# Attention heads and key-value products of a small vision tower in 32-column array tiles, one for each pair of heads

## The reference, cut to what matters

```python
# local branch: a band of 12 tokens around each token
qk = einsum('bhsd,bhswd->bhsw', fmap(q), fmap(k_windowed))
out_local = einsum('bhsw,bhswd->bhsd', qk, v_windowed) / clip(qk.sum(-1), 1e-6)
# strided branch: every third token (the global branch: all tokens, read through 12 anchor queries)
kv = einsum('bhsd,bhse->bhde', k_s, v_s)
out_stride = einsum('bhsd,bhde->bhse', fmap(q), kv) / norm
# out = wl * out_local + ws * out_stride + wg * out_global, then a linear layer
```

## Time and profile before

| | us |
|---|---|
| median of 3 runs | 257.41 (256.68 to 260.4) |
| the profiled execution | 256.9 |
| span of its trace | 255.1 |
| attention steps 4 to 8 in the trace (66.44 to 134.97) | 68.5 |
| step 9 (134.97 to 144.10) | 9.1 |

### The profile page before, as it was taken

One profiled execution on the slowest core, in us unless ns is written; L12 is line 12 of the kernel. 1 busy time (PEld: TensorE's weight loads), 2 busy tenths in 40 slices (PEclk: granted clock), 3 DMA queues, 4 the chain that ended last, 5 costly groups with the idle time before them and its releaser, 6 DMA issues.

```text
span 255.1 us, 4433 instructions
## 1 busy us (share of the span) xinstructions
PE 219.5 (86%) x1340; PEld 189.2 (74%) x1340; DVE 141.2 (55%) x422; ACT 110.8 (43%) x252; POOL 74.7 (29%) x109
## 2 busy tenths in 40 slices
PE   7397797995999999999999773599999999999940
PEld 6286496663887967878879561489999999999930
DVE  5345248696567858657456459765776433424200
ACT  2334366864143443735326595245433424334210
POOL 4003350372004060413322363002332423324240
PEclk9659599996799999999795555579999999999996
DMA  7999999999500000000100596532342342431313
GB/s 131 188 234 159 262 291 270 265 215 255 195 10 0 0 4 1 0 3 0 31 4 26 172 318 163 134 95 49 52 59 39 57 54 37 67 44 18 31 15 89
DMA packets 26259, 25.73 MB, mean 101 GB/s; under 512 B 4971, under 2 KB 23262, under 8 KB 26222
## 3 DMA queue, kind: packets, MB, share of 16 engines
q1 hardware_dynamic: 22333, 22.17, 35.6%
q0 software_dynamic: 3568, 2.64, 8.2%
q10 hardware_dynamic: 336, 0.66, 1.5%
HBM read 16.57 MB, written 7.77 MB: 95 GB/s over the span
## 4 chain that ended last, share of the span: by engine, by line
PE 73%; DVE 8%; DMA 7%; ACT 4%; issue 3%; SPq 2%; POOL 1%; DVEq 0%; ACTq 0%; POOLq 0%
PE ps L973 12%; PE ps L950 12%; PE ps L708 7%; PE ps L712 6%; PE ps L798 5%; PE ps L580 4%; PE ps L784 4%; PE ps L962 4%; PE ps L677 4%; DMA ximg<-in_x 3%; PE ps L691 2%; PE ps L681 2%; DMA sent<-row,index 1%; PE ps L572 1%; DMA sums<-ys,xs 1%
## 5 line engine op out<-in xcount | busy, mean ns | idle before, releaser
L1640 POOL DMA_INDIRECT sums<-ys,xs x17 | 26.3, 1546 | 66.6 <-ACT ys L1537 57.1
L973 PE MATMUL ps<-w2s,hidT 128*128 x204 | 36.1, 327 | 1.1 <-DVE hidT L1341 0.8
L973 PEld LDWEIGHTS ps<-w2s,hidT 128*128 128x128 f32 x204 | 33.0, 189 | 2.1 <-issue 1.6
L950 PE MATMUL ps<-w1hi,xhi 128*128 x68 | 25.3, 372 | 1.0 <-ACT xend L1530 0.7
L1537 ACT ACTIVATE ys<-ps,xs 128x192 f32<-128x192 f32 x17 | 7.2, 421 | 39.9 <-PE ps L973 37.6
L1320 DVE TENSOR_TENSOR xlo<-ps,xhi 128x128 fp32r<-128x128 f32 x17 | 5.0, 292 | 28.2 <-ACT xend L1530 28.2
L1627 POOL COPY vexp<-vtok 114x32 f32<-114x32 f32 (+1 forms) x36 | 8.0, 222 | 42.6 <-PE ps L712 40.6
L1419 ACT ACTIVATE qlb<-ps,cst 96x228 f32<-96x228 f32 (+1 forms) x36 | 12.1, 426 | 16.8 <-PE ps L746 16.8
L1147 DVE TENSOR_TENSOR kvb<-ps,cst 96x288 f32<-96x288 f32 (+1 forms) x24 | 10.0, 418 | 16.1 <-PE ps L784 16.1
L708 PE MATMUL ps<-at,vexp 114*96 114x114 f32 (+1 forms) x144 | 18.7, 286 | 0.0
L784 PE MATMUL ps<-vm,ktok 114*96 114x288 f32 (+1 forms) x48 | 15.6, 406 | 2.7 <-DVE kvb L1147 2.7
(11 more groups left out here) (192 smaller groups left out, 473.1 us busy)
## 6 DMA issues: line engine op xcount, KB each, us to landing
w2s<-in_L_ffn_W SPq DMA_DIRECT2D x8, 576.0 KB
sent<-blank SPq DMA_DIRECT2D x1, 3977.0 KB, 32.5
w1s<-in_L_ffn_W SPq DMA_DIRECT2D x4, 768.0 KB, 16.6
xs<-sent SPq DMA_DIRECT2D x17, 96.0 KB, 2.0
w1s<-in_L_ffn_W SPq DMA_DIRECT2D x4, 384.0 KB, 18.1
w1hi<-w1hi SPq DMA_DIRECT2D x8, 192.0 KB
ximg<-in_x SPq DMA_DIRECT2D x12, 96.0 KB, 7.9
w1s<-in_L_ffn_b SPq DMA_DIRECT2D x1, 792.0 KB
```

The costliest lines, as they stand in the source:

```text
L950: last = pe.matmul(ps[2 + c][:, 0:PASS], xx, of_expert(ww, expert), start=(n == 0), stop=(n == len(products) - 1))
L973: last = pe.matmul(ps[6 + j % 2][:, 0:D], hidT[:, k, :], of_expert(w2s[:, :, k, :], expert), start=(k == 0), stop=(k == FCH - 1))
L1640: po.indirect_dma_start(sums, bass.IndirectOffsetOnAxis(ap=xs[:, j % NS, D + TAIL + 1:].bitcast(U32), axis=0), ys[:, j % 2, :], None, comp ...
```

## The change

The heads are taken in pairs: 32 channels, `PAIRS = 3` in each half of 96.

- `keys_values(g, i)`: for a half, three products instead of two. Product `r` loads the 32 key columns of pair `r`, streams the masked values of the same pair for both branches and three images (2 x 3 x 32 = 192 columns) and writes rows 32r to 32r+31 of `ps[5]`. It is issued at parts 0 and 2 of a step and no longer at parts 1 and 3. For the last group it streams 192 columns as well, where it was 96.
- `own_blocks(g, i)`: three VectorE instructions of 32 rows for a half, where there were two of 96 rows. The blocks of `kvb` outside the pairs are set to zero once, by a new GpSimd memset (`gp_blocks_zero`).
- `outputs(g, i)`: `vexp` is 32 columns wide. Six products as before, but each loads 32 columns and writes the 32 rows of its pair; the three first heads of the pairs are issued first, then the three second heads, which are summed on them. The products with `kvb` that follow stay as they are, 96 columns in the full tile.
- GpSimd fills `vexp` in two copies of 96 values instead of six of 32, and clears 768 values in place of 2304.

`scores` and the linear outputs are as they were.

```diff
+TW = 2 * HD
+PAIRS = HALF // TW
...
-        vm = sb("vm", [GTOK, 2, 2, 2 * PER, HALF])
+        vm = sb("vm", [GTOK, 2, 2, PAIRS, 2 * PER, TW])
...
-        vexp = sb("vexp", [GTOK, 2, HEADS, HALF])
+        vexp = sb("vexp", [GTOK, 2, HEADS, TW])
...
-                for hh in range(HH):
-                    pe.matmul(o, vexp[0:n, g % 2, i * HH + hh, :], at[0:n, g % 2, i * HH + hh, 0:w],
-                              start=(hh == 0), stop=False, skip_group_check=True)
+                for a in range(2):
+                    for r in range(PAIRS):
+                        hh = i * HH + 2 * r + a
+                        pe.matmul(ps[7][TW * r:TW * (r + 1), i * GTOK:i * GTOK + w], vexp[0:n, g % 2, hh, :],
+                                  at[0:n, g % 2, hh, 0:w], start=(a == 0), stop=False, skip_group_check=True)
...
-            def keys_values(g, m):
-
-                t0, n, imgs = group(g)
-                i, kind = m // 2, m % 2
+            def keys_values(g, i):
+
+                n = group(g)[1]
                 pe.wait_ge(gp_masked_values, 2 * g + i + 1)
-                if 4 * g + m >= 1:
-                    pe.wait_ge(dv_keys_values, 4 * g + m)
-                pe.matmul(ps[5][0:HALF, 0:imgs * HALF], ktok[0:n, g % KS, i * HALF:(i + 1) * HALF],
-                          vm[0:n, g % 2, i, kind * PER:kind * PER + imgs, :],
-                          start=True, stop=True).then_inc(pe_keys_values, 1)
+                if 2 * g + i >= 1:
+                    pe.wait_ge(dv_keys_values, 2 * g + i)
+                for r in range(PAIRS):
+                    c = i * HALF + r * TW
+                    last = pe.matmul(ps[5][TW * r:TW * (r + 1), 0:2 * PER * TW], ktok[0:n, g % KS, c:c + TW],
+                                     vm[0:n, g % 2, i, r].rearrange("p k c -> p (k c)"), start=True, stop=True)
+                last.then_inc(pe_keys_values, 1)
...
-                        keys_values(t - 3, m)
+                        if m % 2 == 0:
+                            keys_values(t - 3, m // 2)
                         scores(t - 3, m)
...
-                ve.tensor_tensor(kvb[:, g % 2, i, kind * PER:kind * PER + imgs, :],
-                                 ps[5][0:HALF, 0:imgs * HALF].rearrange("p (b c) -> p b c", c=HALF),
-                                 blk.unsqueeze(1).broadcast_to([HALF, imgs, HALF]), ALU.mult).then_inc(dv_keys_values, 1)
+                for r in range(PAIRS):
+                    c = slice(TW * r, TW * (r + 1))
+                    last = ve.tensor_tensor(
+                        kvb[c, g % 2, i, :, c].rearrange("p (k b) c -> p k b c", b=PER)[:, :, 0:imgs],
+                        ps[5][c, 0:2 * PER * TW].rearrange("p (k b c) -> p k b c", b=PER, c=TW)[:, :, 0:imgs],
+                        blk[c, c].unsqueeze(1).unsqueeze(1).broadcast_to([TW, 2, imgs, TW]), ALU.mult)
+                last.then_inc(dv_keys_values, 1)
...
+                    link(po.memset(kvb[:], 0.0), gp_blocks_zero)
                     link(po.memset(vexp[:], 0.0), gp_vexp_zero)
```

More of the change, by code:

```diff
@@ L406, in build @@
         gp_vexp_zero = sem("gp_vexp_zero")
+        gp_blocks_zero = sem("gp_blocks_zero")
         gp_masked_values = sem("gp_masked_values")
@@ L697, in outputs @@
                 w = max(n, HALF)
[L698 removed]
+                pe.wait_ge(dv_keys_values, 2 * g + 2)
                 pe.wait_ge(dv_windows, 4 * g + 4)
[L700 removed]
+                pe.wait_ge(gp_head_values, 2 * (g + 1))
                 pe.wait_ge(ac_from_anchors, g + 1)
@@ L1138, in over_anchors, with own_blocks @@
                                      r[:, i, :].unsqueeze(2).broadcast_to([HA, imgs, SEQ]), ALU.mult).then_inc(dv_anchored, 1)
-            def own_blocks(g, m):
-                t0, n, imgs = group(g)
+            def own_blocks(g, i):
+                imgs = group(g)[2]
                 if g >= 2:
                     ve.wait_ge(pe_heads, g - 1)
-                ve.wait_ge(pe_keys_values, 4 * g + m + 1)
-                i, kind = m // 2, m % 2
-                ve.tensor_tensor(kvb[:, g % 2, i, kind * PER:kind * PER + imgs, :],
-                                 ps[5][0:HALF, 0:imgs * HALF].rearrange("p (b c) -> p b c", c=HALF),
-                                 blk.unsqueeze(1).broadcast_to([HALF, imgs, HALF]), ALU.mult).then_inc(dv_keys_values, 1)
+                else:
+                    ve.wait_ge(gp_blocks_zero, 1)
+                ve.wait_ge(pe_keys_values, 2 * g + i + 1)
+                for r in range(PAIRS):
[5 more added lines that the diff above has]
+                last.then_inc(dv_keys_values, 1)
             def windows(g, m):
@@ L1227, in _ @@
                     if 0 <= t - 3 < GROUPS:
-                        own_blocks(t - 3, m)
+                        if m % 2 == 0:
+                            own_blocks(t - 3, m // 2)
                         windows(t - 3, m)
@@ L1625, in _ @@
                     po.wait_ge(pe_heads, g - 1)
-                for hh in range(HH):
+                for a in range(2):
                     link(po.tensor_copy(
-                        vexp[0:n, g % 2].rearrange("p (i a) c -> p i a c", i=2)[:, :, hh, hh * HD:(hh + 1) * HD],
-                        vtok[0:n, g % 3].rearrange("p (i c) -> p i c", i=2)[:, :, hh * HD:(hh + 1) * HD]), gp_head_values)
+                        vexp[0:n, g % 2].rearrange("p (r a) c -> p r a c", a=2)[:, :, a, a * HD:(a + 1) * HD],
+                        vtok[0:n, g % 3].rearrange("p (r c) -> p r c", c=TW)[:, :, a * HD:(a + 1) * HD]), gp_head_values)
             po.wait_ge(sent_blank, 16)
```

17 lines of the change are left out of this document (8 added, 9 removed).

## The result

The changed kernel takes 268.02 us, the median of four runs (266.03 to 273.94), beside 258.9 (256.68 to 263.39) for the kernel before; the ratio is 1.0388, 95% interval 1.0336 to 1.044. That is slower, and outside the range I gave. Now and then an execution comes out some per cent longer than the others of its kernel, and the ratios in this document leave such executions out, so a ratio is not always the quotient of the two medians. The profiled execution is the longest of the four, 273.94 us, with the granted clock (PEclk on the page, in tenths of full speed) at 0.50 in the first part of step 4 too; a second one (`after_again`, 265.45 us, span 263.6) stands closer to the other three, and I read the steps from it.

What follows compares the result with a forecast made beforehand. TensorE's stream was taken to bound steps 4 to 8. Terms -0.3 + 0 + 0.1 - 1.1 = -1.3 us on 256.9 gave 255.6, 256.1 as median, forecast 256; 8-in-10 range 249.5 to 266.5.

Steps and rivals of the forecast that it cites:

- The bound: Steps 4 to 8: bound by order and length of TensorE's stream, VectorE some 4 us a step behind.
- What one pass costs: Heads and key-value products: partly overlapping tiles save 0.49 us a heads block, 0.33 a key-value half, 1.64 a step.
- full overlap: Rival: second passes of heads and key-values also run side by side, 6.9 us less than forecast, 249 us; chance 0.20.
- What the tile changes cost: TensorE entering and leaving 32-column tiles: 0.29 us a visit, four visits, 1.16 us a step.
- VectorE and the new wait: Fourth `scores` waits for `windows` behind three `own_blocks`: 0.3 to 0.5 us, 0.4 taken, a step.
- Steps 4 to 7: Saving, tile changes and new wait together: -0.1 us a step, -0.3 in four.
- Step 3: TensorE's wait moves to the fourth `scores`, idle nearly 4 us in place of 2.65; nothing gained or lost.
- Steps 8 and 9: Last attention steps: +0.1 us in the first, -1.1 us in the second, which runs at half clock.
- The clock: Rival: more low-clock stretches at 3.1 us each, two giving 262.3 us, a third 265; chance 0.10.

Runs made afterwards that it cites:

- heads_only: Kernel before with only the heads in 32-column tiles (new `vexp`, copies and `outputs`), key-value products as they were: 251.0 us, ratio 0.9749.
- heads_by_pair: Kernel before with only the heads in 32-column tiles, loops exchanged so both products of one tile follow each other: 255.64 us in one run.
- keys_only: Changed kernel with `vexp`, its copies and the heads' loop as before, so only key-values are in 32-column tiles: 262.64 us, ratio 1.0163.
- after_fill6: Changed kernel with three dense products that nobody reads at the end of step 6, nothing else: 262.97 us, ratio 1.0218.
- whole_filled: Changed kernel with second half's `own_blocks` behind fourth `windows`, plus unread products: four in step 3, two ending step 6, one ending steps 7 and 8: 246.86 us.
- after_filled: Changed kernel plus unread dense products, four in step 3, one ending each of steps 6, 7, 8: 251.04, 251.69, 251.77, 267.34, 267.42 us.
- after_relit: Changed kernel with six dense products that nobody reads in step 7, behind `outputs` of the first half, no other filling: 268.96 us, ratio 1.0308.
- blocks_behind: Changed kernel with the second half's `own_blocks` behind the fourth `windows` in VectorE's queue: 264.02 us, ratio 1.0232.
- before_idle: Kernel before with two VectorE instructions without effect ahead of the residual of step 6, so TensorE waits longer: 262.47 us, ratio 1.0116.

## Why the prediction was wrong, step by step

**The bound.** Right: TensorE's stream sets steps 4 to 8, and what it saves in step 5 of `heads_only` comes off the step without remainder.

**What one pass costs.** Here a term was mis-sized. I let the tiles overlap by one pass only and took seven pass times, 0.69 us, for the heads and four, 0.65, for the key-values. No run shows these two terms: the products take 0.52, and 0.46 to 0.49, and these have the way into the tile in them, which I had put into another term. Without it the heads take 0.39 by four of the pass times of the earlier trace rows (4 x 0.098, an estimate), which is 0.30 less than I took. Of the rivals, full overlap was the right one for these rows. The second L713 block of step 5 in windows of 0.05 to 0.06 us, only the matmuls of that line, first profile:

```profile
91.60:91.65 0.05, 0.05 (x3) 0.05 (x6) 1.00 0.00 0
91.68:91.74 0.06, 0.06 (x6) 0.06 (x5) 1.00 0.00 0
91.78:91.84 0.06, 0.06 (x9) 0.06 (x5) 1.00 0.00 0
```

Three passes are under way, then six, then nine (a pass has 262 ns in its record and the next one starts before it ends): they start three at a time. The start times of the records say the same: 91.54, 91.66, 91.76 and 91.86, at each of them three within 13 to 14 ns. In the kernel before the passes of the heads start one by one, 0.1 us apart, and a window of this length has four under way:

```profile
69.40:69.45 0.05, 0.05 (x4) 0.05 (x3) 1.00 0.00 0
```

The rows do not name the tile; that the three are one for each tile is the reading that fits, as `heads_by_pair` has the same threes with both products of a tile in succession. By that reading each tile goes through its own four passes, 4 x 0.098 = 0.39 us, and the 0.13 that is left of 0.52 goes to entering the tile; both are estimates. With the tile change in it the block is 1.18 / 0.52 = 2.3 times as fast at 114 streamed columns. With an overlap of one pass only, six products would have taken seven pass times, 0.69 us.

**What the tile changes cost.** Right in size. I took 0.29 us a visit, from products with 38 loaded columns in step 5, which the earlier trace rows show slower than those with 114 in step 4: 1.41 us for 1.29 in L677, and 0.54 for 0.39 in L770 behind it. No row or run names the tile of either; that the 0.27 us in all are the price of another tile was my estimate. The heads show 0.52 - 0.39 = 0.13 on the way in, an estimate as the 0.39 is, and 1.35 - 1.18 = 0.17 on the way out, 0.30. By step: 2 x (1.18 - 0.39 - 0.30) = 0.98 us, and `heads_only` has 0.97.

**VectorE and the new wait.** The mechanism was right, the size too small. I wrote 0.3 to 0.5 us a step, 0.4 taken. It is 0.74, 0.51 (0.17 + 0.34) and 0.97 in steps 4, 5 and 6. Two terms carry it. In step 4, three `own_blocks` start 0.36 us apart (75.83, 76.19, 76.55), not 0.26 as the pair I had taken from the earlier trace rows, so `windows` starts 1.11 us behind the first of them and not 0.78. Each of the four starts only when the one ahead has ended (an `own_blocks` takes 0.35 us), where the second of the pair in the earlier trace rows starts before the first has ended, and so does `windows` behind `own_blocks` in the kernel before (60.19, with 0.44 us from 59.83 on). The three work on rows 0, 32 and 64 and the pair on the same rows; no run tells whether that is why. (Those 0.3 to 0.5 us have an estimate of 0.24 in them for the time from the end of streaming to VectorE's start, which no run shows; here the last pass of L790 starts at 75.38 and the first `own_blocks` at 75.83, which by 0.162 us a pass leaves 0.29, an estimate.) And in step 6 VectorE itself is late, which I had left out; its timeline there, second profile:

```profile
102.71 0.15 DVE L1200 MAX8 top<-logit 114x8 f32<-114x8 f32 x1
...
103.67 0.15 DVE L1207 TENSOR_TENSOR diff<-top 114x1 f32<-114x1 f32 x1
103.79 1.08 DVE L1157 TENSOR_TENSOR kvb<-ps,cst 32x192 f32<-32x192 f32 x3
104.90 0.52 DVE L1167 TENSOR_TENSOR at<-ps,cst 114x342 f32<-114x342 f32 x1
```

The choice of experts, 1.1 us of small instructions, stands ahead of the three `own_blocks`. By `keys_only`, the key-value tiles' own gain is 0.53 us of work in step 5, and the wait takes it all.

**Steps 4 to 7.** -0.1 us a step forecast; -0.7 to -0.9 in steps 4 to 6, because of the overlap. The wait was larger than forecast and the overlap more than paid for it. Step 7 is the clock's.

**Step 3.** The wait moved to `scores` and became 4.25 us, near the "nearly 4" forecast; the step is 0.7 us longer, not even.

**Steps 8 and 9.** I forecast +0.1 and -1.1; together they are 2.2 us longer. The clock is at 0.50 there for 0.71 before, so the two terms do not show by themselves.

**The clock.** This is where the forecast fell. I had a falling clock among the rivals, with the right sign, but gave it 0.10 and priced it by one row: two or three more stretches of 6.8 us at 3.1 us each, 262 to 265. That the clock falls where streaming thins out was a guess of mine; the earlier trace rows show only a clock of 0.50 in step 9, where TensorE reads busy throughout, and 0.50 behind the wait of step 3. The step that failed is this price: it assumed that a low stretch ends after 6.8 us as the one at 59.9 in the kernel before does. In the changed kernel it lasts 68.3 us, up to the expert layer. In step 7 that is 20.05 us for 12.07 (`after_fill6`), 8.0 us, and in steps 8 and 9 23.5 for 16.9 (`whole_filled`), 6.6: some 15 us together, an estimate across kernels, of which the kernel before also pays a part. The executions of one program, `after_filled`, fall into two groups 16 us apart, with the clock.

What the runs show of the cause: with dense products at the thin places and the other order on VectorE the loss is gone (`whole_filled`, 246.86 us), with one product at each place in three executions of five (`after_filled`); among dense products the clock came back at 128.4 us, with the narrow tiles there (`after_relit`); with VectorE's order alone repaired it still fell, at 108.5 us (`blocks_behind`), and with the end of step 6 alone filled at 127.6 us, behind step 7 (`after_fill6`); and it also fell, once, at 112.7 us, behind a longer wait with full tiles (`before_idle`). In these traces it takes both halves of the change to stay down so long: with either half alone the clock fell at the same place (107.2 and 115.2 us) and came back after 6.8 us. That the low clock is what the change loses is shown; why the fall comes just at the end of step 6 is not, since the heads alone had it there without a new wait. By the pass times, heads and key-values have 2 x 0.39 + 2 x 0.32 = 1.4 us of streaming in a step with both, where they had 2 x 1.18 + 4 x 0.49 = 4.3, while TensorE reads busy 19.5 of 20.05 us in step 7. That the missing streaming is what keeps the clock down is an argument from these numbers and from `after_relit`; no run varies it step by step, so it stays open.

## What to carry to other kernels

Shortening the streaming of the engine that bounds this kernel cost more than it saved: 0.7 to 0.9 us a step were gained in steps 4 to 6, and 10.0 us lost from step 7 on, at a granted clock of 0.50. So look at the granted clock of each stretch before and after, and price a fall by the distance to the next dense work (here the expert layer, where the stretches of 30 us and more ended), not by the shortest low stretch in the old trace. Take such a change apart and keep the half that pays by itself: the heads alone give 0.975, and 0.949 with four dense products in step 3 and one in each of steps 6 to 8 whose result nobody reads; the filling alone brings the kernel before to 254.92 from 259.49. Look, too, at where a traced execution stood before the first touched instruction: here that alone moved by several microseconds. Where a saving on one engine puts work in one piece on the engine behind it (six instructions in two groups of three), the wait that this makes belongs in the sum at the spacing of three in a row (0.36 us here), not of a pair (0.26).

## What the runs showed of the hardware that I had not expected

- Passes of float32 products that load 32 columns each, for three different blocks of 32 rows, start three at a time (91.54, 91.66, 91.76, 91.86 us in the first profile): six products in 0.52 us for 1.18, and 0.54 with both products of a block in succession.
- Three VectorE instructions of 32 rows and 192 values out of PSUM start 0.36 us apart, each when the one ahead has ended, where two of 114 rows that follow each other in the kernel before start 0.26 apart, the second before the first has ended.
- The granted clock stays at 0.50 while TensorE reads busy 97% of step 7 (19.54 of 20.05 us in the second profile), so the busy share of the profile does not tell the clock. In `after_relit` it came back at 128.4 us, among products of 384 streamed columns; in the same step with full tiles it came back after 6.8 us in `before_idle`.
- One program can have two times: `after_filled` took 251.0 to 251.8 us in three runs, at a mean clock of 0.881 to 0.903, and 267.3 to 267.4 in two, at 0.817 and 0.835.
